# A four-layer graph network on one Trainium2 core: one-hots of two attention passes made by ScalarE, an indirect scatter without its index bound, and a block of zero rows written later

## The reference, cut to what matters

```
L0: msgs = edge_weight * (h @ weight)[dst];  agg = segment_sum(msgs, src)        then batch norm and relu
L1: out  = segment_sum((h @ weight[rel])[src, edge_type], dst)
L2: alpha = leaky_relu(h[src]·a_src + h[dst]·a_dst)  per head (8 heads)
    out   = segment_sum(softmax over the edges of a dst (alpha) * h[src], dst)
L3: scores = Q[dst]·K[src] * 0.25 + edge_features @ We + be
    out    = segment_sum(softmax over the edges of a dst (scores) * V[src], dst) @ Wo + bo
```

## Time and profile before

| | us |
|---|---|
| runs (3): median, lowest, highest | 4916.95, 4915.68, 4922.77 |
| profiled execution: its own time | 4933.33 |
| its span | 4931.6 |
| POOL busy | 3239.5 (66%) |
| PE busy | 3108.3 (63%) |
| DVE busy | 2379.7 (48%) |
| ACT busy | 924.0 (19%) |

### The profile page before, as it was taken

How to read it: one execution, slowest core, us unless ns; L and a number is a source line. 1 busy time by engine, 2 the same in 40 slices (tenths; PEclk the granted TensorE clock), 3 DMA queues, 4 the chain that set the end, 5 groups by cost and what they waited for, 6 DMA issues and landing times.

```text
span 4931.6 us, 58738 instructions
## 1 busy us (share of the span) xinstructions
PE 3108.3 (63%) x17717; PEld 2647.6 (54%) x17717; DVE 2379.7 (48%) x5597; ACT 924.0 (19%) x2143; POOL 3239.5 (66%) x3283
## 2 busy tenths in 40 slices
PE   6765444554496444344445888887885777777776
PEld 5654333444493333333334777776773565666664
DVE  9742222222374000100003666666665888888886
ACT  3211111110002443333331111111111111111111
POOL 2267777777400777777774777777772777777773
PEclk7565777655698555555555777778777899899998
DMA  3511111111482111111111222222221333333332
GB/s 100 174 43 52 52 51 51 50 50 50 157 298 115 53 53 52 50 53 53 53 53 48 55 55 54 55 55 55 55 54 50 102 99 100 100 100 100 100 101 61
DMA packets 162124, 377.42 MB, mean 77 GB/s; under 512 B 59963, under 2 KB 72132, under 8 KB 160892
## 3 DMA queue, kind: packets, MB, share of 16 engines
q0 software_dynamic: 118656, 276.72, 19.4%
q1 hardware_dynamic: 38706, 94.06, 5.4%
q10 hardware_dynamic: 4474, 2.92, 0.2%
HBM read 292.49 MB, written 83.61 MB: 76 GB/s over the span
## 4 chain that ended last, share of the span: by engine, by line
POOL 57%; issue 19%; PE 13%; DVE 7%; DMA 3%; DVEq 1%; POOLq 0%; ACT 0%; ACTq 0%; SPq 0%
POOL work L625 26%; POOL work L609 16%; POOL msgs L594 15%; PE banks L1011 4%; PE banks L844 2%; PE banks L808 1%; PE banks L827 1%; PE banks L919 1%; PE banks L834 1%; DMA work<-kv_table,idx_a 1%; PE banks L909 1%; DVE scores L1279 1%; DVE acc L1188 1%; DVE acc L1281 1%; DMA work<-gat_table,idx_a 1%
## 5 line engine op out<-in xcount | busy, mean ns | idle before, releaser
L609 POOL DMA_INDIRECT work<-rel_table,idx_b x808 | 770.8, 954 | 543.4 <-DMA rel_table<-work 297.4
L625 POOL DMA_INDIRECT work<-kv_table,idx_a x808 | 820.7, 1016 | 296.2 <-issue 241.2
L625 POOL DMA_INDIRECT work<-gat_table,idx_a x808 | 800.4, 991 | 291.1 <-issue 242.0
L594 POOL DMA_INDIRECT msgs<-work,idx_a x808 | 786.2, 973 | 291.2 <-issue 244.6
L1059 PE MATMUL banks<-work,arena 128*128 128x128 f32 x1616 | 414.8, 438 | 591.7 <-DMA work<-rel_table,idx_b 583.4
L1059 PEld LDWEIGHTS banks<-work,arena 128*128 128x128 f32 x1616 | 356.6, 325 | 656.0 <-issue 656.0
L1000 PE MATMUL banks<-nodes,work 128*128 x1616 | 355.4, 389 | 458.7 <-DVE work L1502 458.7
L844 PE MATMUL banks<-work,arena 128*128 128x136 f32 x3232 | 564.3, 328 | 58.7 <-DVE work L1210 56.5
L1000 PEld LDWEIGHTS banks<-nodes,work 128*128 128x128 f32 x1616 | 305.5, 283 | 525.6 <-issue 525.6
L844 PEld LDWEIGHTS banks<-work,arena 128*128 128x128 f32 x3232 | 506.7, 231 | 124.3 <-issue 113.9
L682 ACT ACTIVATE attr<-banks 128x512 f32<-128x512 f32 x404 | 241.2, 597 | 1450.3 <-PE banks L819 1450.3
(11 more groups left out here) (300 smaller groups left out, 4618.7 us busy)
## 6 DMA issues: line engine op xcount, KB each, us to landing
work<-msgs SPq DMA_DIRECT2D x101, 516.0 KB, 4.6
msgs<-work,idx_a POOLq DMA_INDIRECT x808, 2.3
work<-rel_table,idx_b POOLq DMA_INDIRECT x808, 2.5
work<-gat_table,idx_a POOLq DMA_INDIRECT x808, 2.5
work<-kv_table,idx_a POOLq DMA_INDIRECT x808, 2.7
rel_table<-work SPq DMA_DIRECT2D x25, 512.0 KB, 2.6
attr<-in_edge_attr SPq DMA_DIRECT2D x50, 250.0 KB
rec<-work SPq DMA_DIRECT2D x1, 6400.0 KB, 18.4
```

The source lines that it names most:

```text
L594: nc.gpsimd.indirect_dma_start(msgs, bass.IndirectOffsetOnAxis(ap=idx_a[:, t:t + 1], axis=0), msg_ring[:, t % SPAN, :], None, bounds_check ...
L609: nc.gpsimd.indirect_dma_start(row_ring[:, t % SPAN, :], None, rel_table, bass.IndirectOffsetOnAxis(ap=idx_b[:, t:t + 1], axis=0)).then_in ...
L625: nc.gpsimd.indirect_dma_start(ring[:, t % SPAN, :], None, table, bass.IndirectOffsetOnAxis(ap=idx_a[:, t:t + 1], axis=0)).then_inc(quad_i ...
```

## The change

It has three parts.

- In both attention passes DVE's `hot` is gone, with the iota copy in PSUM. ACT makes the one-hots in `soft_out` instead, with the two steps of the L1 pass: three quads ahead of the loop, then in each body `apart(q + 3)` before `turn_out(q + 2)` and `together(q + 3)` behind it.
- The tensor `msgs` is twice as long, the message scatter has no bound on its indices, and a place that was skipped now has an index of its own in the upper half, `PLACES + p * T + t`. DVE works this out with `tile_no`.
- The plain DMA for the tail's zero rows, with the wait for the 25 small scatters ahead of it, moves behind the gathers of the groups on POOL.

```diff
-        msgs = dram("msgs", [PLACES, MSG])
+        msgs_all = dram("msgs", [2 * PLACES, MSG])
+        msgs = msgs_all[0:PLACES, :]
...
-            pool.wait_ge(gap_out, 16 * NB)
-            pool.dma_start(msgs.rearrange("(p t) w -> p t w", t=T)[:, MG_T:T, :],
-                           rep(bn[:, :, :].rearrange("p a f -> p (a f)")[:, 0:MSG], T - MG_T)).then_inc(tail_out, 16)
             pool.wait_ge(flag_set, 1)
...
                     bounds_check=GROUPS - 1, oob_is_err=False).then_inc(group_in[c], 16)
 
+            pool.wait_ge(gap_out, 16 * NB)
+            pool.dma_start(msgs.rearrange("(p t) w -> p t w", t=T)[:, MG_T:T, :],
+                           rep(bn[:, :, :].rearrange("p a f -> p (a f)")[:, 0:MSG], T - MG_T)).then_inc(tail_out, 16)
             pool.wait_ge(tail_out, 16)
             for q in range(NQ_FULL):
                 pool.wait_ge(quad_rdy, q + 1)
                 for t in range(QUAD * q, QUAD * (q + 1)):
                     nc.gpsimd.indirect_dma_start(
-                        msgs, bass.IndirectOffsetOnAxis(ap=idx_a[:, t:t + 1], axis=0),
-                        msg_ring[:, t % SPAN, :], None, bounds_check=PLACES - 1, oob_is_err=False)\
-                        .then_inc(quad_out[q % QUADS], 16)
+                        msgs_all, bass.IndirectOffsetOnAxis(ap=idx_a[:, t:t + 1], axis=0),
+                        msg_ring[:, t % SPAN, :], None).then_inc(quad_out[q % QUADS], 16)
...
+                def apart(q):
+
+                    if q >= QUADS:
+                        act.wait_ge(agg, at_agg[ph] + QUAD * (q + 1 - QUADS))
+                    for t in range(QUAD * q, QUAD * q + QUAD):
+                        ins = nc.scalar.activation(span_oh[:, q % QUADS, t % QUAD, :], iota[:, :], ACT.Abs,
+                                                   bias=dst_local[:, t:t + 1], scale=-1.0)
+                    ins.then_inc(apart_rdy, 1)
+
+                def together(q):
+
+                    act.wait_ge(apart_rdy, (n - 1) * NQ_FULL + q + 1)
+                    nc.scalar.activation(span_oh[:, q % QUADS, :, :], span_oh[:, q % QUADS, :, :], ACT.Relu,
+                                         bias=ones[:, 0:1], scale=-1.0).then_inc(oh_rdy, 1)
...
+                    if q + 3 < NQ_FULL:
+                        apart(q + 3)
                     if q + 2 < NQ_FULL:
                         turn_out(q + 2)
+                    if q + 3 < NQ_FULL:
+                        together(q + 3)
...
+                for q in range(3):
+                    apart(q)
+                    together(q)
                 turn_out(0)
                 turn_out(1)
                 steps(body)
...
-                def hot(q, row):
-
-                    V.tensor_tensor(span_oh[:, q % QUADS, :, :], rep(row, QUAD),
-                                    bc(dst_local[:, QUAD * q:QUAD * q + QUAD], P), ALU.is_equal).then_inc(oh_rdy, 1)
-
...
-                    if q + 3 < NQ_FULL:
-                        if q + 3 >= QUADS:
-                            dve.wait_ge(agg, at_agg[ph] + QUAD * (q + 4 - QUADS))
-                        hot(q + 3, iota[:, :] if k == 0 and i else iota_bank)
...
-                dve.wait_ge(h_out, (n + 1) * NB)
-                V.tensor_copy(iota_bank, iota[:, :])
                 drain()
-                for q in range(3):
-                    hot(q, iota_bank)
...
+            V.tensor_scalar(vio[:, 1:2], node_no[:], float(T), float(PLACES), ALU.mult, ALU.add)
+            drain()
+            V.tensor_scalar(tile_no, tile_no, vio[:, 1:2], None, ALU.add)
             for i in range(0, 4 * TC, 2):
                 field_out(V.tensor_copy, dve, i)
...
-            V.scalar_tensor_tensor(fields[:, 0, :], fields[:, 0, :], -float(PLACES), map_tmp, ALU.add, ALU.mult)
-            drain()
-            V.tensor_scalar(idx_a[:, 0:T], fields[:, 0, :], float(PLACES), None, ALU.add).then_inc(tiles_set, 1)
+            V.tensor_tensor(fields[:, 0, :], fields[:, 0, :], tile_no, ALU.subtract)
+            drain()
+            V.tensor_tensor(fields[:, 0, :], fields[:, 0, :], map_tmp, ALU.mult)
+            drain()
+            V.tensor_tensor(idx_a[:, 0:T], fields[:, 0, :], tile_no, ALU.add).then_inc(tiles_set, 1)
```

More of the change, by code:

```diff
@@ L226, in gnn @@
         quad_sums = psA[:, 4:8, 0:F + HEADS]
-        iota_bank = banks[:, 0, P:2 * P]
         quad_bases = maps[:, 0:N_BASES].rearrange("p (c v) -> p c v", v=QUAD + 1)
```

## The result

The changed kernel takes 4901.6 us (median of 11 runs, 4894.6 to 4907.5), the kernel before 4928.3 us in the 11 runs beside it: ratio 0.9945, 95% interval 0.9935 to 0.9955, some 27 us less (22 to 32). Run again later, the ratio was 0.9943 (0.9925 to 0.9961). Forecast were 41 us less, and 4876 us; 4901.6 lies in the range given, 1.4 us under its upper end. The profiled execution takes 4902.1 us, its span 4900.1 (before 4933.3 and 4931.6).

The account below looks back on a forecast made before the run. POOL's issue of 808 indirect DMAs in each of four stages was taken to bound the kernel. Front -5.6, scatter -23.4 and passes -12 sum to -41 us: 4917 - 41 = 4876 us, range 4846 to 4903.

Parts of the forecast that it names:

- Passes: L2 and L3 attention passes: one-hots on ACT end 24 us of POOL stalls, half given back to weighting L1210: -12 us.
- quads with k = 1: Attention passes: L1210 falls at a fixed moment for each k, so more quads with k = 1 are caught than now.
- Scatter: Message scatter: without the bound each of 808 DMAs saves 0.029 us, 23.4 us less; 0 and 36 kept as bounds.
- the bound was free: Rival on the message scatter: it stays at 0.97 us without the bound, kernel 4899 us; chance 0.14.
- Front: Before the first scatter: moving the tail DMA gives -7.1 us, added index arithmetic +1.5, together -5.6 us.
- the first scatter: Sign at the front's end: POOL's first message scatter starts at 262 instead of 267.7 us.
- the end of PE's wait at L909: Sign in the front: PE no longer waits 5.86 us at L909 for an `attr` load.
- the means of the gathers: Sign in the attention passes: the two L625 groups fall from 991 and 1016 to about 985 and 1000 ns.
- the scatter's mean: Sign in the message scatter: L594's mean is 944 instead of 973 ns, its stage 1008 us instead of 1031.
- The stalls only move: Rival on the attention passes: L1210 takes over all stalls the one-hots caused, -29 us, kernel 4888; chance 0.11.
- The lock onto POOL's starts: Rival on the attention passes: L1210 could hold POOL in every quad, up to 0.50 us each, +79 us, 4996; chance 0.06.
- the emptied grid: Rival on the attention passes: DVE's slack puts L1210 between POOL's starts, stalls halve and more, kernel 4833; chance 0.09.

Follow-up runs that it names:

- point 3: Kernel before with the one-hots of both attention passes made by ACT, scatter and tail as before: ratio 0.9966 (0.9954 to 0.9977), 17 us faster.
- the quarter: Kernel before with only the one-hots from SBUF (every fourth quad) moved to ACT, the others on DVE from PSUM: ratio 0.9983, 8 us faster.
- points 6 and 7: Changed kernel, weighting reading ACT's second copy of the weights for three of four quads: from PSUM, ratio 0.9840; from SBUF, on a third chip, 0.9962.

## Why the prediction was nearly right

**Passes: right in kind and in size, wrong in where the stalls went.** "I give half back: -12". Measured -14 by the pages, -17 (11 to 23) by the times of point 3. The one-hots' stalls went (24 forecast, 21 measured), and the weighting took 10 of them over (12 forecast). I expected quads with k = 1 to be caught more. They hardly are: the DMAs of over 1.00 us with a weighting of k = 1 inside them are 41 in a page before and 48 after (means, both passes), where it is 19 and 50 for k = 0, 32 and 75 for k = 2, 55 and 30 for k = 3. And a part of the old stalls was of another kind: in the L3 pass, DVE ran one-hot, addition and weighting without a gap in quads with k = 2, and a DMA of POOL that started 0.23 us ahead of the weighting was held until after it, 24 times in the first page:

```profile
4002.93 0.67 DVE L1110 TENSOR_TENSOR arena<-banks,dst_local 128x512 f32<-128x512 f32 x1
...
4003.53 0.70 DVE L1188 TENSOR_TENSOR acc<-acc,banks 128x544 f32 x1
4003.93 1.73 POOL L625 DMA_INDIRECT work<-kv_table,idx_a  x1 [0.30 <-issue]
4004.16 0.67 DVE L1210 TENSOR_TENSOR work<-work 128x512 f32<-128x512 f32 x1
```

DMAs that start in the addition have an excess of 8 to 19 us in the L3 pass in the four pages with one-hots on DVE, the quarter's included, and under 0.5 us in the five with ACT's; the weighting alone rises there from 13 to 20 us to 29 to 39. That "half" came out is in part luck, then: the account by k and the chain was not the one forecast. The first comparison, 25 us less, would have made this term look mis-sized; it was one long page of the L3 pass (1065.5, against 1057.8 and 1053.8 with the same code).

**Scatter: the mis-sized term.** "If the bound is the difference, each of 808 saves 0.029 us": I took the whole distance between a scatter with a bound and a gather without. Half of it is the scatter's own. Measured 0.014 us, of which 0.011 reached the stage: 9 us instead of 23.4. The rival "the bound was free" had 0 and was nearer, 9 us off where the forecast was 14.

**Front: right, with 1 us more.** -8.2 + 1.6 = -6.6 where -7.1 + 1.5 = -5.6 was forecast. Pages in which PE was granted the high clock in the field groups gain 2.5 us more; the forecast did not have that.

**The sum.** In the difference, -41 forecast, -27 (22 to 32) measured. The scatter was 14 us too much, the front and the passes 4.5 us too little (by the means of the pages); the last 4 us between -31 and -27 are within the interval. In the time itself, 4876 forecast and 4901.6 measured, 11 us more come from the three runs that the forecast started from. The range held by 1.4 us only, and it held since its upper end allowed for a free bound. Of the signs named, the first scatter (262.0 at the low clock), the end of PE's wait at L909 and the means of the gathers (983 and 993 for 985 and 1000) came; the scatter's mean (963 for 944) and its stage (1023 us for 1008) didn't.

**The rivals.** "The stalls only move" gave -29, the right time by the wrong reason: it had 6 us for the front, 23 for the scatter and nothing for the passes, where 8, 9 and 14 were measured. The Trainium skill's page "SBUF — State Buffer" (section "Who interferes with whom") infers that `tensor_tensor` leaves descriptor generation alone; the traces of points 6 and 7 disagree, by up to 0.52 us for each DMA that starts in one with both operands in SBUF. The lock onto POOL's starts and the emptied grid didn't come: POOL's excess as a whole is 71 us in the pages with ACT's one-hots, 0.18 us per quad, where it would have decided from 0.30. No gap of POOL that PE's sums ended was over 0.3 us on the first two chips.

## What to carry to other kernels

Where POOL issues the lists of indirect DMAs that bound a stage, look first at which DVE operations have all operands in SBUF: put one operand of the longest into PSUM, before moving others to another engine. Here that was worth 50 us, on a chip where POOL's stalls set the time. Removing a smaller cause of collisions gives part of its worth to the larger one. Price an option of an instruction from the same instruction without it, not from a cousin, and hold two pages of one kernel against each other before a difference of 10 us between pages is explained.

## What the runs showed of the hardware

- A DMA of POOL that starts 0.04 to 0.50 us after the start of a DVE `tensor_tensor` of 128x512 with both operands in SBUF is stalled, by 0.05 to 0.52 us: 62 to 116 such per pass in the weightings of nine traces, 1,579 of 1,579. With one operand in PSUM: none of 1,157 in seven traces (one-hots and weightings), each within 0.014 us of the undisturbed DMA. A DMA that starts within 0.015 us of the operation's start is hardly ever stalled (5 of 189).
- The bound of an indirect scatter costs 0.014 us (0.972 against 0.958), the scatter itself 0.014 more than a gather (0.958 against 0.944).
- The kernel before took 4928 to 4934 us in three comparisons, on two or three chips, and 5507 us on one more. On that one POOL idles about 2 us some hundred times in a pass, released by nothing that the profile names, and four kernels whose stalls differ by up to 91 us in the two passes take the same time for them within 6 us.
- PE's granted clock in two stretches (the field groups, the sums after the last gather) falls on either level from page to page of one kernel; that goes with 2.5 and 8 us.
